# A decoder layer on one core: routing, expert weights and the first chunk's expert products moved into the last turns of the context attention

## The chip, the core and the metric

One core of one Trainium2 chip runs the whole kernel. The metric is the device time of one launch in microseconds (us). The kernel before took 2490.17 us, the median of 3 runs (2486.51 to 2495.47). About 0.3% of it, some 7 us, is what a measurement of this kernel can tell from no change. The engines are called PE (TensorE, with its weight loads PEld), DVE (VectorE), ACT (ScalarE), POOL (GpSimd) and SP (SyncE, which issues all transfers here). Each runs its own list of instructions in order. They wait for each other with semaphores.

## What is computed

For each of 2 batches of 2048 tokens of width 512, three steps follow one another, each added to its input:

```
x = x + attention(layernorm(layernorm(x)))                  # 8 heads of 64, normalised q and k
x = x + context_attention(layernorm(x), ctx, ctx)           # 16 heads of 32, 128 context tokens
h = layernorm(x)
idx = top_2(h[:, 0, :] @ Wr + br)                           # two of 8 experts, chosen by token 0 of the batch
x = x + mean over k of (gelu(h @ W1[idx_k] + b1[idx_k]) @ W2[idx_k] + b2[idx_k])
```

All is float32. The kernel splits each operand of a large product into a high and a low float16 part and adds three products, high x high, high x low and low x high. The two experts are the same for all tokens of a batch, and they depend on token 0 of its first chunk alone.

## The kernel before, in words

`decoder_layer` loops over the batches (`nc.Fori(0, B)`). A batch has five stages, each an `nc.Block` in which every engine has its list: projections of the self attention, its scores and values, a short stage that prepares the context's keys and values, the context attention, and the experts. The change touches the last two.

**The context attention** (from L1067) works on 4 chunks of 512 tokens (`CH`), each 4 tiles of 128 (`TPC`). It is a software pipeline of bodies `body(c)`, c = 0 to 4, written out without a loop, and with a list of its own for each engine. Body c holds the attention of chunk c, the output projection of the self attention and the queries of chunk c+1, and the output projection of chunk c-1. The order in which PE calls the pieces is the order in the list. `transposes(kind, c, j)` (L1257, or L888 for "t5") turns one tile of 128 x 512 into a bank of PSUM with 4 matrix instructions. Kind "t5" is the self attention's output, "t0" the normalised input of the queries, "t2" the context attention's output, "t3" the normalised input of the experts. ACT copies the high half out (`high`, L1503), DVE subtracts for the low half (`low`, L1628). `attn_project`, `query` and `cross_project` are products of 12 matmuls of 128 x 128 by 512 each (`mm3`, L159 to L161), as a rule four of them to a chunk. `maxima` (L1300, L1652) and `max_rows` (L1308) find and place the row maxima of the scores. For each of 4 groups of heads g, `scores(c, g)` (L1324) fills four banks, ACT takes the exponential of each pair twice (`exponentials`, L1541 and L1542), POOL subtracts (`probs_low`, L1153), PE multiplies with the values (`values`, L1340 to L1344) and DVE divides by the sums (`output`, L1665 and L1669). `scores` of the next group waits for that division (`d_o`), as it writes the same four banks. `residual2` (L1635, with statistics L922 and L925) adds a projected tile to x, `norm_scale` (POOL, L910 to L917) and `layer_norm` (ACT, L1510) normalise it for "t3". Two banks (TB) serve the transposes and maxima in turn, two (PB) the projections; the order of turns is written in `T_TURNS` and `P_TURNS`, and each turn waits for the reader of the turn two before.

**The experts** (L1790 to L1943) begin when that block has ended. DVE adds the two halves of token 0's column (L1906), PE multiplies with the router's weights (L1841), DVE adds the bias and finds the two largest (L1908 to L1914), SP reads the two indices into registers (L1801) and only then issues the weights: four matrices of 512 x 512, two for `w1` and two for `w2`, in 8 pieces of 128 x 1024 (`load_pieces`, L132), through four slots of `stage_f`. For each piece ACT writes the high half (`split_high`, L140), DVE the low half (`split_low`, L148). Pieces 0 to 3 are the `w1` matrices. The second biases are added to x on POOL (L1835). Then, for each chunk, PE makes 8 products of 12 matmuls from the chunk's "t3" tiles (L159 to L161), ACT takes the gelu (L1894), DVE splits the result into `gh` (L1930) and `gl` (L1932), and PE makes 4 tiles of 24 matmuls each (L1871 to L1875), which DVE adds to x (L1943) and SP writes out. In chunk 0 the splitting of pieces 2 to 7 stands between the gelus; `pe.Fori(0, CH)` runs over the chunks.

## Time and profile before

| | us |
|---|---|
| median of 3 runs (lowest, highest) | 2490.17 (2486.51, 2495.47) |
| the profiled execution, its own time | 2491.35 |
| its span, first to last instruction | 2489.7 |
| PE busy | 2236.2 (90%) |
| DVE, ACT, POOL busy | 1553.7, 1614.5, 1486.8 |
| batch 2: last bodies 2 to 4 of the context attention | 2176.6 to 2294.8 |
| batch 2: routing and first weights | 2294.8 to 2307.3 |
| batch 2: experts of chunk 0, of chunks 1 to 3 | 2307.3 to 2361.8, to 2486.2 |

A row of the profile names the line of the kernel, the engine, the operation, and output <- input. In a line of the timeline the first number is the start in us from the span's start, the second the duration, and the brackets behind it the idle time of the engine before it and who ended that. Matmuls overlap: one of 512 columns is shown with 0.38 us, while the next starts 0.22 us after it. PEclk (and "clock") is the granted clock of TensorE as a share of 2.4 GHz; its two levels are 1.2 GHz (0.50) and 2.4 GHz (1.00), and a stretch shows their mean.

### The profile page before, as it was taken

Reading aid. Unit: us, or ns where it says so; the run is one execution under the profiler, and the core shown is the slowest. Engines: PE = TensorE matmul, PEld = TensorE weight load, DVE = VectorE, ACT = ScalarE, POOL = GpSimd, SP = SyncE. Lnnn points to the kernel's source line nnn. Section 1 sums busy time; section 2 is a strip of 40 time slices with the busy share of each in tenths; the row PEclk is TensorE's granted clock in tenths of the full one; section 3 lists DMA queues with packets and bytes.
Section 4 is the critical chain, followed back from the end, with each engine's and each line's share of the span. In section 5 each row is a group of like instructions: output and inputs, shape, how many; then the busy total and the mean of one; then the engine's idle time right before and its main releaser. Section 6 shows DMA issues by size and latency. Waiting matters only on the chain. (4 is left out here: it accounts for less than half of the span.)

```text
span 2489.7 us, 65787 instructions
## 1 busy us (share of the span) xinstructions
PE 2236.2 (90%) x22384; PEld 1272.3 (51%) x22384; DVE 1553.7 (62%) x2583; ACT 1614.5 (65%) x1828; POOL 1486.8 (60%) x978
## 2 busy tenths in 40 slices
PE   6988999999996899589969889999999968995899
PEld 3544666666663455334435446666666634553344
DVE  6986777777755566353269867777777555663532
ACT  4555999999995556421045469999999945564210
POOL 3325898988985676340033258988989956763400
PEclk9998999999998999789979889999999979997899
DMA  4220000000003000020042200000000030000300
GB/s 102 56 38 1 10 2 6 9 9 8 9 9 106 10 2 2 18 77 17 34 107 56 34 2 10 9 0 9 9 8 9 9 115 1 2 1 15 80 17 34
DMA packets 103502, 65.14 MB, mean 26 GB/s; under 512 B 76498, under 2 KB 76498, under 8 KB 103378
## 3 DMA queue, kind: packets, MB, share of 16 engines
q1 hardware_dynamic: 103378, 63.57, 12.1%
q8 instruction: 68, 1.11, 0.2%
q14 instruction: 56, 0.46, 0.1%
HBM read 46.69 MB, written 8.39 MB: 22 GB/s over the span
## 5 line engine op out<-in xcount | busy, mean ns | idle before, releaser
L668 POOL TENSOR_TENSOR probs_l<-probs,probs_h 128x1024 f16<-128x1024 f32 x448 | 980.4, 2215 | 166.1 <-PE bank L720 127.6
L789 DVE TENSOR_REDUCE pm<-bank 128x1 f32<-128x512 f32 x1024 | 680.5, 688 | 276.8 <-PE bank L676 272.4
L772 ACT ACTIVATE probs_h<-bank,shift 128x1024 f16<-128x1024 f32 x512 | 569.4, 1112 | 51.9 <-PE bank L692 51.9
L780 ACT ACTIVATE probs<-bank,shift 128x1024 f32<-128x1024 f32 x512 | 572.6, 1118 | 34.6 <-DVE probs_l L803 30.3
L691 PE MATMUL bank<-q_hh,ko 128*128 (+1 forms) x1024 | 392.0, 383 | 29.5 <-DMA q_lm<-nm 17.1
L676 PE MATMUL bank<-ko,q_hh 128*128 (+1 forms) x1024 | 397.0, 391 | 21.0 <-PEq L313 12.4
L692 PE MATMUL bank<-q_lm,k_h 65*128 (+1 forms) x1024 | 392.0, 383 | 0.0
L705 PEld LDWEIGHTS bank<-v_hl,probs_h 128*128 128x128 f16 x4096 | 288.1, 98 | 66.3 <-issue 8.3
L705 PE MATMUL bank<-v_hl,probs_h 128*128 (+1 forms) x4096 | 320.8, 192 | 0.8 <-ACT probs_h L772 0.8
L707 PE MATMUL bank<-v_hl,probs_h 128*128 (+1 forms) x4096 | 318.8, 193 | 0.0
L707 PEld LDWEIGHTS bank<-v_hl,probs_h 128*128 128x128 f16 x4096 | 268.1, 96 | 59.1 <-issue 0.5
L720 PEld LDWEIGHTS bank<-v_hl,probs_l 128*128 128x128 f16 x4096 | 187.2, 97 | 57.3 <-POOL probs_l L668 5.1
L1894 ACT ACTIVATE g<-bank,b1c 128x512 f32<-128x512 f32 x64 | 44.1, 689 | 260.5 <-PE bank L161 244.9
L720 PE MATMUL bank<-v_hl,probs_l 128*128 (+1 forms) x4096 | 207.6, 193 | 4.6 <-POOL probs_l L668 4.6
L390 POOL TENSOR_SCALAR rs_a<-mv_a 128x1 f32<-128x1 f32 x32 | 6.2, 192 | 318.4 <-DMA lnb<-in_L_attn_ln_beta 181.7
L1153 POOL TENSOR_TENSOR pxl<-px,pxh 128x1024 f16<-128x1024 f32 x64 | 135.2, 2132 | 58.8 <-ACT px L1542 58.6
L676 PEld LDWEIGHTS bank<-ko,q_hh 128*128 (+1 forms) x1024 | 100.3, 98 | 126.2 <-DVE pm L789 33.4
L691 PEld LDWEIGHTS bank<-q_hh,ko 128*128 (+1 forms) x1024 | 99.7, 97 | 94.6 <-DMA q_lm<-nm 18.1
L692 PEld LDWEIGHTS bank<-q_lm,k_h 65*128 (+1 forms) x1024 | 99.9, 98 | 65.0 <-issue 3.0
L159 PE MATMUL bank<-x2th,fwh_w 128*128 x256 | 100.9, 394 | 29.3 <-DVE fwl_w L148 29.3
L475 ACT ACTIVATE sq<-bank 128x512 f32<-128x512 f32 x64 | 38.3, 599 | 120.8 <-PE bank L161 120.8
L1652 DVE TENSOR_REDUCE nmt<-bank 128x4 f16<-128x512 f32 x128 | 81.7, 692 | 55.5 <-PE bank L1300 54.6
(204 smaller groups left out, 4157.8 us busy)
## 6 DMA issues: line engine op xcount, KB each, us to landing
xt_a<-in_x SPq DMA_DIRECT2D x32, 256.0 KB, 2.7
q_lm<-in_x SPq DMA_DIRECT2D x32, 256.0 KB, 4.6
stage_f<-in_L_ffn_W SPq DMA_DIRECT2D x32, 256.0 KB, 4.8
out<-yt_f SPq DMA_DIRECT2D x32, 256.0 KB, 2.0
q_hh<-q_hh SPq DMA_DIRECT2D x32, 128.0 KB, 2.5
ko<-k_h SPq DMA_DIRECT2D x32, 128.0 KB, 2.7
q_lm<-nm SPq DMA_DIRECT2D x256, 0.2 KB, 4.9
v_hl<-in_L_attn_w_q SPq DMA_DIRECT2D x8, 256.0 KB, 7.0
```

The source lines that it names most:

```text
L159: pe.matmul(bank, xh(c), wh(c), start=(c == 0), stop=False)
L668: pool.tensor_tensor(probs_l[:, p % 2, :], probs[:, p % 2, :], probs_h[:, p % 4, :], ALU.subtract).then_inc(pl_pool, 1)
L676: pe.matmul(MB[k % 2], qf[:, bass.ds(r * CT + k // 4 * P, P)], k1[:, bass.ds(r // CH * N + k % 4 * CT, CT)], start=True, stop=True)\
L691: pe.matmul(bank, k1[:, kcols], qf[:, qcols], start=True, stop=False)
L692: mm = pe.matmul(bank, k2[0:DH + 1, kcols], lf[0:DH + 1, qcols], start=False, stop=True)
L705: pe.matmul(ob[:, o0:o0 + DH + 1], rows, vf[:, bass.ds(v0, DH + 1)], start=(p == 0 and half == 0 and t == 0), stop=False, skip_group_check ...
L707: pe.matmul(ob[:, o0:o0 + DH], rows, vf[:, bass.ds(v0 + DH + 2, DH)], start=False, stop=False, skip_group_check=True)
L720: mm = pe.matmul(ob[:, o0:o0 + DH + 1], probs_l[:, p % 2, half * CT + t * P:half * CT + t * P + P], vf[:, bass.ds(v0, DH + 1)], start=Fals ...
L772: act.activation(probs_h[:, p % 4, :], SB[p % 2][:, :], ACT.Exp, bias=shift[:, 0:1]).then_inc(ph_ready, 1)
L780: act.activation(probs[:, p % 2, :], SB[p % 2][:, :], ACT.Exp, bias=shift[:, 0:1]).then_inc(p_ready, 1)
L789: dve.tensor_reduce(pm[:, s, k:k + 1], MB[k % 2], AX_X, ALU.max).then_inc(mx_free, 1)
L1153: pool.tensor_tensor(pxl[:, k % 2, :], px[:, k % 2, :], pxh[:, k % 2, :], ALU.subtract)\
```

## The change

The block of the experts is gone. Its work stands in the lists of the context attention. Bodies 0 and 1 stay as they are; bodies 2 to 4 are replaced by one list for each engine, in which are interleaved:

- the column of token 0, the routing product (`route`) and the choice (`column`, `choose`) near the beginning of body 2's work, since chunk 0's "t3" tiles are ready by then;
- the loads of the weights, by SP, once the last "t5" transpose has read the self attention's output: its memory between the outputs of the chunks holds `stage_f`, `b2r` and `b2s` (`o_gap`). The split halves go where dead matrices and tiles lie (`fwh`, `fwl`: the weights "o" and "xq", and `oth`, `otl`, `xth`, `xtl`), and wait therefore for the last attention projection (pieces 0 to 3) or the last query (4 to 7);
- the 8 first products of chunk 0 (`expert_up`) on PE: one behind `values(3, 1)`, two behind `scores(3, 2)`, two behind `scores(3, 3)`, one behind `values(3, 6)`, two behind `values(3, 7)`. They share the banks PB with the projections. DVE copies each from its bank to float32 in memory (`expert_raw`, new work), and ACT takes the gelu from there, after all exponentials, so that its tables are loaded once a batch as before;
- the 4 second products of chunk 0 (`expert_down`) behind the last projection, and the last three "t3" transposes behind these. The loops of all engines then run over chunks 1 to 3. Before its loop PE waits for the low half of the last "t3" tile (`d_tl`).
- On POOL, three of four additions of the second bias for chunk 0 (`add_b2`) stand between `norm_scale(1, 2, 1)` and `probs_low(3, 2)`; `query_low(3, 3)` stands behind `probs_low(3, 3)`, `add_xbo(3, 2)` and `add_xbo(3, 3)` behind `probs_low(3, 7)`. The additions for chunks 1 to 3 wait for `gl` of the chunk before.

The diff, cut to its core (indented less than in the file):

```diff
+b2r = [o_gap(i, 2 * D, D) for i in range(2)]
+b2s = [o_gap(2 + i, 2 * D, D) for i in range(2)]
+fwh = {"w10": wh["o"], "w11": oth, "w20": wh["xq"], "w21": xth}
+fwl = {"w10": wl["o"], "w11": otl, "w20": wl["xq"], "w21": xtl}
+g32 = q32
+raw = [tok0, tokx[0]]
+yt = [bo_b, xbo_b]
+def gh(k, ec):
+    return raw[k][:, ec, :].bitcast(F16)[:, 0:CT]
+def gl(k, ec):
+    return raw[k][:, ec, :].bitcast(F16)[:, CT:2 * CT]
 SB = banks[0:4]
 TB = banks[4:6]
...
+    sp.wait_ge(d_t_done, T_BASE + t_of("t5", CH - 1, TPC - 1) + 1)
+    sp.nop(nofuse=True)
+    load_pieces(sp, b, PIECES_P4[:4], stage_f, src)
+    for k in range(2):
+        sp.dma_start(b1c[:, k, :], b1[bass.ds(expert[k], 1), :, :].rearrange("a p c -> p (a c)"))\
+            .then_inc(f_b, 16)
+        sp.dma_start(b2r[k], b2[bass.ds(expert[k], 1), :].broadcast_to([P, D])).then_inc(f_b, 16)
+    load_pieces(sp, b, PIECES_P4[4:], stage_f, src)
+    with sp.Fori(0, CH) as c:
...
+    def add_b2(c, j):
+        n = b * CH + c
+        pool.wait_ge(f_b2, 2 * b + 2)
+        pool.wait_ge(d_n1, n * TPC + j + 1)
+        pool.tensor_tensor(x2_tile(c, j), x2_tile(c, j), b2s[1], ALU.add).then_inc(f_xb, 1)
...
+    add_b2(0, 3)
+    norm_scale(pool, 1, 3, 3)
+    pool.wait_ge(d_n1, (b * CH + CH) * TPC)
+    pool.nop(nofuse=True)
+    with pool.Fori(1, CH) as c:
+        n = b * CH + c
+        pool.wait_ge(f_gl, n * 8)
...
+    def route():
+        pe.wait_ge(r_col, b + 1)
+        bank = bank_free("rt", 0, 0)
+        for d in range(DC):
+            mm = pe.matmul(bank[0:1, 0:E], col[:, d:d + 1], wr_sb[:, d, :], start=(d == 0),
+                           stop=(d == DC - 1))
+        mm.then_inc(r_mm, 1)
+    def expert_up(w):
+        k, ec = w // DC, w % DC
+        if w == 0:
+            pe.wait_ge(d_tl, T_BASE + t_of("t3", 0, TPC - 1) + 1)
+        if ec == 0:
+            pe.wait_ge(w_split, pieces_split(b, PIECES_P4[:2 * k + 2]))
+        ecols = slice(ec * P, ec * P + P)
+        mm3(pe, bank_free("f1", 0, w), lambda d: fwh[f"w1{k}"][:, d, ecols],
+            lambda d: fwl[f"w1{k}"][:, d, ecols], lambda d: x2th[:, d, 0:CT],
+            lambda d: x2tl[:, d, 0:CT]).then_inc(f1_done, 1)
+    def expert_down(n, j):
+        if j == 0:
+            pe.wait_ge(d_o, (b * CH + CH) * 8)
+            pe.wait_ge(w_split, pieces_split(b, PIECES_P4))
+        pe.wait_ge(f_y, n * TPC + j + 1)
+        cols = slice(j * P, j * P + P)
+        bank = SB[j % 2][:, :]
+        for w in range(8):
+            k, ec = w // DC, w % DC
+            if j == 0:
+                pe.wait_ge(f_gl, n * 8 + w + 1)
+            pe.matmul(bank, gh(k, ec)[:, cols], fwh[f"w2{k}"][:, ec, :], start=(w == 0),
+                      stop=False)
+            pe.matmul(bank, gh(k, ec)[:, cols], fwl[f"w2{k}"][:, ec, :], start=False, stop=False)
+            mm = pe.matmul(bank, gl(k, ec)[:, cols], fwh[f"w2{k}"][:, ec, :], start=False,
+                           stop=(w == 7))
+        mm.then_inc(f2_done, 1)
...
+    max_rows(3)
+    transposes("t2", 2, 1)
+    scores(3, 0)
+    cross_project(2, 0)
+    cross_project(2, 1)
+    transposes("t2", 2, 2)
+    transposes("t2", 2, 3)
+    values(3, 0)
+    values(3, 1)
+    expert_up(0)
+    scores(3, 1)
+    cross_project(2, 2)
+    transposes("t3", 2, 0)
+    cross_project(2, 3)
+    values(3, 2)
+    values(3, 3)
+    transposes("t3", 2, 1)
+    scores(3, 2)
+    expert_up(1)
+    expert_up(2)
+    values(3, 4)
+    transposes("t3", 2, 2)
+    values(3, 5)
+    transposes("t3", 2, 3)
+    scores(3, 3)
+    expert_up(3)
+    expert_up(4)
+    values(3, 6)
+    expert_up(5)
+    values(3, 7)
+    expert_up(6)
+    transposes("t2", 3, 0)
+    expert_up(7)
+    transposes("t2", 3, 1)
+    cross_project(3, 0)
+    transposes("t2", 3, 2)
+    transposes("t2", 3, 3)
+    cross_project(3, 1)
+    cross_project(3, 2)
+    transposes("t3", 3, 0)
+    cross_project(3, 3)
+    expert_down(b * CH, 0)
+    expert_down(b * CH, 1)
+    expert_down(b * CH, 2)
+    expert_down(b * CH, 3)
+    transposes("t3", 3, 1)
+    transposes("t3", 3, 2)
+    transposes("t3", 3, 3)
+    pe.wait_ge(d_x2, (b * CH + CH) * TPC)
+    pe.wait_ge(f_raw, b * 8 + 8)
+    pe.wait_ge(d_tl, T_BASE + len(TILES))
+    pe.nop(nofuse=True)
...
+    def weights_high(p):
+        if p < 4:
+            act.wait_ge(d_o_done, (b * CH + CH) * TPC)
+        else:
+            act.wait_ge(d_q_done, (b * CH + CH) * DC)
+        split_high(act, b, PIECES_P4[p:p + 1], stage_f, fwh)
+    def gelu(w):
+        k, ec = w // DC, w % DC
+        if w == 0:
+            act.wait_ge(d_ql, (b * CH + CH) * DC)
+            act.wait_ge(f_b, b * 64 + 64)
+        act.wait_ge(f_raw, b * 8 + w + 1)
+        if w >= 2:
+            act.wait_ge(f_gl, b * (CH * 8) + w - 1)
+        act.activation(g32[:, w % 2, :], raw[k][:, ec, :], ACT.Gelu, bias=b1c[:, k, ec:ec + 1],
+                       scale=INV_WS).then_inc(f_g, 1)
...
+    exponentials(3, 0)
+    exponentials(3, 1)
+    high("t2", 2, 2)
+    high("t2", 2, 3)
+    weights_high(7)
+    layer_norm(1, 2, 0)
+    exponentials(3, 2)
...
+    exponentials(3, 6)
+    exponentials(3, 7)
+    high("t3", 2, 3)
+    act.preload_act_table(ACT.Gelu)
+    gelu(0)
+    gelu(1)
+    gelu(2)
+    gelu(3)
+    high("t2", 3, 0)
+    gelu(4)
+    high("t2", 3, 1)
+    gelu(5)
+    high("t2", 3, 2)
+    gelu(6)
+    layer_norm(1, 3, 0)
+    gelu(7)
+    high("t2", 3, 3)
+    layer_norm(1, 3, 1)
+    layer_norm(1, 3, 2)
+    high("t3", 3, 0)
+    high("t3", 3, 1)
+    high("t3", 3, 2)
+    layer_norm(1, 3, 3)
...
+    def column():
+        dve.wait_ge(d_tl, T_BASE + t_of("t3", 0, 0) + 1)
+        dve.tensor_tensor(col[:, :], x2th[:, :, 0], x2tl[:, :, 0], ALU.add).then_inc(r_col, 1)
+    def choose():
+        dve.wait_ge(r_mm, b + 1)
+        dve.tensor_tensor(sc[:, :], proj_bank("rt", 0, 0)[0:1, 0:E], br_sb[:, :], ALU.add)\
+            .then_inc(r_sc, 1)
+        dve.wait_ge(r_sc, b + 1)
+        dve.nop(nofuse=True)
+        dve.max(best[:, :], sc[:, :]).then_inc(r_top, 1)
+        dve.wait_ge(r_top, b + 1)
+        dve.nop(nofuse=True)
+        dve.max_index(idx[:, :], best[:, :], sc[:, :]).then_inc(r_idx, 1)
+    def weights_low(p):
+        if p < 4:
+            dve.wait_ge(d_o_done, (b * CH + CH) * TPC)
+        else:
+            dve.wait_ge(d_q_done, (b * CH + CH) * DC)
+        split_low(dve, b, PIECES_P4[p:p + 1], stage_f, fwh, fwl)
+    def bias2():
+        dve.wait_ge(f_b, b * 64 + 64)
+        dve.tensor_tensor(b2s[0], b2r[0], b2r[1], ALU.add).then_inc(f_b2, 1)
+        dve.wait_ge(f_b2, 2 * b + 1)
+        dve.tensor_scalar(b2s[1], b2s[0], 0.5, None, ALU.mult).then_inc(f_b2, 1)
+    def expert_raw(w):
+        k, ec = w // DC, w % DC
+        if w == 0:
+            dve.wait_ge(d_t_done, T_BASE + t_of("t0", CH - 1, TPC - 1) + 1)
+        elif w == 4:
+            dve.wait_ge(d_t_done, T_BASE + t_of("t3", CH - 2, TPC - 1) + 1)
+        dve.wait_ge(f1_done, b * (CH * 8) + w + 1)
+        dve.tensor_copy(raw[k][:, ec, :], proj_bank("f1", 0, w)).then_inc(f_raw, 1)
+    def expert_split(n, w):
+        k, ec = w // DC, w % DC
+        dve.wait_ge(f_g, n * 8 + w + 3)
+        dve.tensor_copy(gh(k, ec), g32[:, w % 2, :]).then_inc(f_gh, 1)
+        dve.wait_ge(f_gh, n * 8 + w + 1)
+        dve.tensor_tensor(gl(k, ec), g32[:, w % 2, :], gh(k, ec), ALU.subtract).then_inc(f_gl, 1)
+    def result(n, c, j):
+        cols = bass.ds(c * (TPC * D) + j * D, D)
+        dve.wait_ge(f2_done, n * TPC + j + 5)
+        dve.wait_ge(f_xb, n * TPC + j + 1)
+        dve.wait_ge(y_out[j % 2], n * 32 + 16 * (j // 2) + 16)
+        dve.wait_ge(d_xb, (b * CH + CH) * TPC)
+        dve.wait_ge(d_xb2, (b * CH + CH) * TPC)
+        dve.scalar_tensor_tensor(out=yt[j % 2][:, :], in0=SB[j % 2][:, :], scalar=0.5 * INV_WS,
+                                 in1=x2[:, cols], op0=ALU.mult, op1=ALU.add).then_inc(f_y, 1)
...
+    maxima(3, 15)
+    low("t2", 2, 0)
+    low("t2", 2, 1)
+    bias2()
+    weights_low(3)
+    residual2(2, 0)
+    residual2(2, 1)
+    low("t2", 2, 2)
+    output(3, 0)
+    output(3, 1)
+    weights_low(4)
+    low("t2", 2, 3)
+    expert_raw(0)
+    weights_low(5)
+    residual2(2, 2)
+    output(3, 2)
+    output(3, 3)
+    residual2(2, 3)
+    expert_raw(1)
+    low("t3", 2, 0)
+    weights_low(6)
+    low("t3", 2, 1)
+    output(3, 4)
+    output(3, 5)
+    expert_raw(2)
+    low("t3", 2, 2)
+    weights_low(7)
+    expert_raw(3)
+    low("t3", 2, 3)
+    expert_raw(4)
+    output(3, 6)
+    expert_split(b * CH, 0)
+    expert_raw(5)
+    output(3, 7)
+    expert_split(b * CH, 1)
+    expert_split(b * CH, 2)
+    expert_raw(6)
+    low("t2", 3, 0)
+    expert_split(b * CH, 3)
+    expert_raw(7)
+    low("t2", 3, 1)
+    expert_split(b * CH, 4)
+    residual2(3, 0)
+    low("t2", 3, 2)
+    expert_split(b * CH, 5)
+    residual2(3, 1)
+    low("t2", 3, 3)
+    expert_split(b * CH, 6)
+    expert_split(b * CH, 7)
+    residual2(3, 2)
+    residual2(3, 3)
+    result(b * CH, 0, 0)
+    result(b * CH, 0, 1)
+    low("t3", 3, 0)
+    low("t3", 3, 1)
+    low("t3", 3, 2)
+    result(b * CH, 0, 2)
+    result(b * CH, 0, 3)
+    low("t3", 3, 3)
```

## Rows read from the trace of the kernel before

**Rows 1.** The page: busy time of PE, and its granted clock in 40 slices.

```profile
PE 2236.2 (90%) x22384; PEld 1272.3 (51%) x22384; DVE 1553.7 (62%) x2583; ACT 1614.5 (65%) x1828; POOL 1486.8 (60%) x978
...
PEclk9998999999998999789979889999999979997899
```

**Rows 2.** Windows: length, busy us (and instructions) of each engine, clock.

```profile
core 0: us, PE busy (x) PEld busy (x) DVE busy (x) ACT busy (x) POOL busy (x), PEclk, DMA share, GB/s
2176.60:2229.80 53.20, 50.02 (x469) 27.43 (x466) 35.34 (x70) 33.42 (x47) 34.98 (x41) 1.00 0.01 2
2229.80:2267.50 37.70, 25.46 (x292) 14.44 (x292) 15.61 (x35) 22.86 (x29) 18.74 (x19) 0.82 0.00 1
2267.50:2294.80 27.30, 19.64 (x128) 11.22 (x128) 12.77 (x24) 7.58 (x12) 6.66 (x14) 0.75 0.00 1
2294.80:2307.30 12.50, 0.37 (x9) 0.26 (x9) 3.31 (x8) 2.43 (x3) 0.00 (x0) 0.50 0.65 161
2307.30:2339.20 31.90, 24.91 (x96) 10.22 (x97) 26.62 (x21) 12.15 (x15) 26.09 (x16) 0.87 0.36 86
2339.20:2361.80 22.60, 22.60 (x97) 9.93 (x98) 3.89 (x7) 0.00 (x0) 0.00 (x0) 0.92 0.10 36
2361.80:2486.20 124.40, 124.29 (x576) 56.13 (x574) 35.17 (x60) 16.52 (x24) 0.00 (x0) 1.00 0.07 25
930.70:1116.30 185.60, 144.33 (x1096) 73.91 (x1095) 99.09 (x164) 78.59 (x106) 87.94 (x90) 0.86 0.12 31
```

**Rows 3.** Waits of PE from 2229.8 to 2312: total us, times, longest.

```profile
PE bank L159 <- DVE fwl_w L148: 11.6, 1, 11.6
PE bank L1340 <- POOL pxl L1153: 10.2, 4, 4.4
PE bank L1324 <- DVE ko L1669: 3.3, 3, 2.0
```

**Rows 4.** Timeline, all engines: one group's turn from scores to the next scores.

```profile
2241.96 0.40 PE L1324 MATMUL bank<-qh,kth 32*128 32x512 f16 x4 [0.45 <-DVE ko L1669]
...
2243.20 1.02 ACT L1541 ACTIVATE pxh<-bank 128x1024 f16<-128x1024 f32 x1 [0.36 <-PE bank L1324]
...
2245.23 4.24 POOL L1153 TENSOR_TENSOR pxl<-px,pxh 128x1024 f16<-128x1024 f32 x2 [0.18 <-ACT px L1542]
...
2251.96 0.42 DVE L1669 TENSOR_TENSOR ko<-bank,rd 128x256 f32<-128x256 f32 x1
...
2252.44 0.40 PE L1324 MATMUL bank<-qh,kth 32*128 32x512 f16 x4 [2.05 <-DVE ko L1669]
```

**Rows 5.** Timeline: last t3 tile, column, first weight piece, table load, first product.

```profile
2292.29 1.11 PE L1257 MATMUL bank<-ident,ko 128*128 128x128 f32 x4 [2.37 <-ACT ko L1510]
...
2294.07 0.69 DVE L1628 TENSOR_TENSOR x2tl<-bank,x2th 128x512 f16<-128x512 f32 x1 [0.70 <-ACT x2th L1503]
2295.07 0.17 DVE L1906 TENSOR_TENSOR col<-x2th,x2tl 128x4 f32<-128x4 f16 x1 [0.31 <-PEq L1076]
...
2302.50 1.06 ACT L140 ACTIVATE fwh_w<-stage_f 128x1024 f16<-128x1024 f32 x1 [8.47 <-DMA stage_f<-in_L_ffn_W]
2306.98 1.28 ACT L1884 ACT_TABLE_LOAD   x1 [1.10 <-DMA b2r<-in_L_ffn_b]
...
2307.28 0.61 PE L159 MATMUL bank<-x2th,fwh_w 128*128 x1 [11.64 <-DVE fwl_w L148]
```

**Rows 6.** Timeline of DVE: the same steps beside POOL's additions, and without them.

```profile
2319.06 1.64 DVE L1932 TENSOR_TENSOR gl<-g,gh 128x512 f16<-128x512 f32 x1
2320.63 2.28 DVE L148 SCALAR_TENSOR_TENSOR fwl_w<-stage_f,fwh_w 128x1024 f16<-128x1024 f32 x1
...
2336.67 0.42 DVE L1930 CAST gh<-g 128x512 f16<-128x512 f32 x1
2337.13 0.69 DVE L1932 TENSOR_TENSOR gl<-g,gh 128x512 f16<-128x512 f32 x1
2337.74 1.22 DVE L148 SCALAR_TENSOR_TENSOR fwl_w<-stage_f,fwh_w 128x1024 f16<-128x1024 f32 x1
```

## Prediction: routing, weights and chunk 0's expert products inside the context attention

> **What bounds the kernel now.** I read the page first: PE is busy 90% of the span, and its clock dips in the same places of both batches [rows 1]. So the question is not which engine is busiest but where PE has no work. The windows answer it [rows 2]. Body 2 is dense: 50.0 of 53.2 us busy at clock 1.00. From `max_rows(3)` to the last exponential (37.7 us) PE is busy 25.5 us at clock 0.82; from there to the last "t3" tile (27.3 us) 19.6 us at 0.75; in routing and loading (12.5 us) hardly at all; the first products of chunk 0 take 31.9 us, its second ones 22.6. Chunks 1 to 3 run at 124.4 us for 576 matmuls, 0.216 us each, with nothing left to gain. From body 2 to the end of chunk 0 batch 2 needs 185.2 us (the first six windows), batch 1 185.6 us (the last window); batch 1 repeats the pattern, so I cost one batch and double.
>
> Why does PE idle there? The waits [rows 3] name three causes. One wait of 11.6 us for the split weights: "t3" must be done, then come column, choice, loads, splits, from 2294.07 to 2307.28 [rows 5]. Four waits, 10.2 us, for POOL's low parts of the exponentials, and three, 3.3 us, for the division. These last two are one chain [rows 4]: scores at 2241.96, exponentials from 2243.20, POOL's two subtractions from 2245.23 for 4.24 us, values, division from 2251.96, next scores at 2252.44: 10.5 us a group, while PE has half of that in work. In chunk 3 no queries follow that could fill it. The third loss is in chunk 0: DVE is busy 26.6 of 31.9 us, since beside POOL's 26.1 us of additions its steps are stretched, a weight split 2.28 us against 1.22, a `gl` 1.64 against 0.69 [rows 6].
>
> **The change, part by part**, with A = body 2's work, B = `max_rows(3)` to the last exponential, C = from there to the first second product (`expert_down`), D = the four second products, E = from their end to the first matmul of chunk 1. Before: A 53.2; B 37.7; the rest 94.3 [rows 2].
>
> *Removed*: 12.5 us of routing and loading, and the 31.9 us of first products as a stage of their own. Their 96 matmuls are 20.7 us of PE work at 0.216.
>
> *A.* PE gains only the routing product, 0.37 us [rows 2]. SP's loads have 16 issues and wait for nothing else in SP's list; before, the first piece was ready for ACT 7.4 us after the column [rows 5], and now 20 us or so of other work covers that. DVE gains the column, 0.17 [rows 5], and a choice of four instructions as small, 0.7, and three splits: 35.3 + 0.9 + 3 x (1.22 to 2.28) = 39.9 to 43.0 us. ACT gains seven high halves at 1.06: 33.4 + 7.4 = 40.8. POOL loses three steps. All stay under 53, but the lists are in order and DVE is what paces the 16 maxima at the end, where two of the splits stand: PE waits behind them. Bounds: nothing, or all three splits at 2.28 less the cover, 6. I take 2.8, so A = 56.0.
>
> *B.* The chain of rows 4 stays. Gain: six products (15.5 us) fill PE, 25.5 us at 0.82 being 20.9 at full clock, so 36.4 of work: the clock should stay at 1.00, worth a us or two in the scores. Cost: `expert_up(0)` lies between `values(3, 1)` and `scores(3, 1)`, 2.6 us where PE waits 2.05 us for the division in any case [rows 4], so 1 us; the other five stand under exponentials and POOL's work, cover of 5 us and more a group. POOL gains three additions (26.1 for 16, 1.6 each) and a `query_low` ahead of chain steps: 18.7 + 4.9 + 1.2 = 24.8 us, but 4.9 in one gap of about 5.5 together with two `norm_scale`: 1 us late, perhaps 3. The additions wait for `bias2` on DVE; behind them in POOL's list waits `probs_low(3, 2)`, behind that `values(3, 2)`. DVE gains five splits, the biases (about 1.1), and copies out of PSUM. The copy is not in the trace; the nearest are DVE's steps out of PSUM of this size at 0.69, and a cast at 0.42 from memory; I take 0.69, five of them 3.5: 15.6 + 1.1 + 3.5 + 5 x (1.22 to 2.28) = 26.3 to 31.6 us, under 40. `weights_high(7)` makes ACT wait for a load that begins after `weights_low(3)`, with `exponentials(3, 2)` behind it: asked for about 5 us into B (my estimate from DVE's list), and ready at most 7.4 us later, as the first piece was behind its column [rows 5]: 12.4 us, against 13.4 us when those exponentials began before (2243.20), so no stall, or up to 2 us. B = 40.0 (38 to 45).
>
> *C.* PE: two products 5.2 us, `cross_project(3, *)` 10.4, five transposes at about 0.6, half of the 1.11 seen at the low clock [rows 5], 2.8: 18.4. DVE: 12.8 us of before, less three low halves (2.1, now in E), and eight splits of gelu at 1.07 from start to start [rows 6], 8.6, and three copies, 2.1: 21.4. ACT loads its table first, 1.28 us [rows 5], which was behind the loads before and is now ahead of `gelu(0)`, with `expert_split(0)` behind it on DVE, and the second products behind that. So DVE sets C, not PE: 21.4 plus the first gelu's latency, 23.0 (21 to 25.5).
>
> *D.* 96 matmuls, 20.7; with a clock step 21.0 (20.8 to 22; before 22.6).
>
> *E.* New, with no cover. PE's loop waits for the last "t3" low half. From that tile's transposes to the end of its low half is 2.5 us (2292.29 to 2294.76) [rows 5]; the third tile's bank waits for the first one's low half, and two results of 0.69 us stand between on DVE. One latency, 2.5, is the lower bound, two with the results 6.4, plus a clock dip the upper. E = 6.0 (4 to 7.5).
>
> *Chunks 1 to 3*: same instructions, 124.4. POOL's additions for them fall under the second products, when DVE splits nothing.
>
> Sum: 56.0 + 40.0 + 23.0 + 21.0 + 6.0 = **146.0** a batch against 185.2 and 185.6: 39.2 and 39.6 less, together 78.8. The profiled execution took 2491.35 us, so 2412.5; the median of the runs lies 1.2 below it: **2411**.
>
> **The Trainium skill.** Beside POOL's additions a split takes 2.28 us, 1.06 more than without [rows 6]. "SBUF — State Buffer", section "Who interferes with whom", says of a DVE instruction with two SBUF inputs beside a GpSimd one that the second to issue "fully blocks until the first finishes". Against this change that rule is the first rival below: the new neighbours are POOL's subtractions, which are longer than its additions. "ScalarE: Activation LUTs", section "What ACT_TABLE_LOAD costs", adds some 1.4 us of drain to the load; the trace shows the load's 1.28 alone, and by the page the estimate of the sum would be 2.8 us more over both batches, 2414.
>
> **Rivals.**
> 1. *POOL and DVE lock each other out.* Each of eight splits waits for a whole subtraction (2.12, half of 4.24 [rows 4]), 17.0 us, and each delays one by 1.22, 9.8 us; 26.8 less the 5.1 in A and B is 21.7 more: 167.7 a batch, 35.4 saved, **2456**. For it: each step beside POOL is about 1 us longer [rows 6]. Against: POOL is idle a third of A and half of B, and the stretch shown there is half of this.
> 2. *The products don't fit among the scores.* All six delay the chain instead of lying beside it: B = 37.7 + 15.5 = 53.2, 159.2 a batch, **2438**. For: each is 2.6 us in an ordered list. Against: waits of 4.4 us stand there [rows 3].
> 3. *PE alone decides.* A 50.4; B and C 20.9 + 14.7 + 20.7 = 56.3; D 20.7; E 2.5: 129.9 a batch, 2379; with a little idle time up to 2394. Against: A left 3 us idle even before, and the sum of DVE in C.
> 4. *Slower than before.* The wait in E lets the clock fall, and it stays at 1.2 GHz over the loop's beginning, where every matmul takes twice 0.216. Such time costs itself again; from 39.4 us of full-speed work on (182 matmuls) the gain is gone. Over the whole of chunk 1 (41.5 us) it is 2.1 a batch too much, **2495**. Before, routing and loading ran at 0.50 for 12.5 us, and yet the next stage had 0.87 [rows 2], so the clock comes back in a few us.
>
> **How the numbers follow.** Forecast 0.73 for 2394 to 2438 without rival 2; rival 2 0.08, near the upper end; rival 1 0.10, above; rival 3 0.07, below; rival 4 0.02. The low ends 53.5 + 38 + 21 + 20.8 + 4 = 137.3 give 96 us less, 2394; the high ends 59 + 45 + 25.5 + 22 + 7.5 = 159.0 give 53 less, 2438. The range leaves out 0.19. Faster by over 0.3% (7 us, what a measurement of this kernel can tell from no change): 0.97; within it 0.01, a part of rival 4's case; slower 0.02.
>
> **What would show it.** In the trace after: no window near clock 0.50 ahead of the experts; the first weight load issued inside body 2's work; group turns of chunk 3 at 10 to 11 us (rival 2: 13); splits at 1.2 to 2.3 us (rival 1: over 3, with POOL's subtractions over 2.13); DVE busy over 85% of C; a gap of about 6 us on PE ahead of chunk 1 (rival 4: matmuls 0.43 us apart long behind it). If A grows by more than 6 us, or C passes 27, my reading of DVE's ordered list was too kind.

## Result: 2413 us, against 2411 forecast

On one chip the changed kernel took 2412.97 us, the median of four runs (2405.34 to 2413.87), and the kernel before 2489.82 (four runs, 2486.51 to 2495.47): a ratio of 0.9682, 95% interval 0.9656 to 0.9709. On another chip the same pair gave 2412.30 and 2495.26, ratio 0.9672 (0.9656 to 0.9688). The time lies inside the forecast range, 2394 to 2438, and 2 us from the forecast value. The profiled execution took 2413.03 us, with a span of 2411.4 against 2489.7.

The page of the changed kernel, first lines and the clock, to be held against [rows 1]:

```profile
PE 2222.3 (92%) x22384; PEld 1264.9 (52%) x22384; DVE 1542.9 (64%) x2599; ACT 1611.7 (67%) x1828; POOL 1481.4 (61%) x978
...
PEclk9997999999999899999979979999999998999999
```

PE's instructions are the same number, and its busy time is 14 us less, the time that matmuls were stretched at the low clock. The rest of the 78 us is, for the most part, waiting that is gone. From [rows 2] and the windows below, batch 2 had 39 us of PE idle between the start of B and the start of chunk 1 (12.2, 7.7, 12.1 and 7.0 in the four windows before the second products), and has 7 now (3.9 in B, 3.3 in E); PE's busy time there fell from 93.0 to 81.0 us.

The windows of batch 2 after, in the order A, B, C, D, E, chunks 1 to 3 (columns as in [rows 2]: us, busy us and instructions of PE, PEld, DVE, ACT, POOL, clock, DMA):

```profile
2138.80:2193.70 54.90, 51.63 (x481) 27.70 (x478) 40.60 (x79) 39.89 (x54) 33.32 (x38) 1.00 0.32 78
2193.70:2233.40 39.70, 35.77 (x345) 18.51 (x344) 25.46 (x43) 23.35 (x30) 25.43 (x23) 0.96 0.05 15
2233.40:2256.20 22.80, 22.80 (x160) 12.19 (x158) 19.98 (x36) 10.91 (x17) 7.38 (x10) 1.00 0.00 1
2256.20:2276.90 20.70, 20.70 (x97) 9.44 (x96) 4.39 (x9) 1.29 (x2) 3.33 (x7) 1.00 0.07 27
2276.90:2281.90 5.00, 1.70 (x13) 1.21 (x11) 3.18 (x5) 2.38 (x4) 2.13 (x2) 0.94 0.16 62
2281.90:2407.60 125.70, 125.68 (x576) 56.69 (x576) 34.48 (x59) 16.49 (x24) 12.66 (x11) 0.99 0.06 25
```

The window with clock 0.50 and the products' window with DVE at 26.6 of 31.9 us [rows 2] have no counterpart. PE is busy in all of C and D. The windows' edges are set by hand; the table has the stages from one event to the next (us), taken from the same start and end instructions in every trace. In the runs it repeats within 0.1 us where neither order nor work was changed, except B, where the clock's dips fall differently (38.4 to 39.75), and chunks 1 to 3 behind an E of 5 us (124.3 to 126.0, last section).

| Stage | before, batch 1 / 2 | forecast | after, both |
|---|---|---|---|
| A | 53.4 / 53.4 | 56.0 | 55.1 |
| B | 36.3 / 37.7 | 40.0 | 39.75 |
| C | 72.1 / 71.7 with routing and first products | 23.0 | 22.55 |
| D | 22.4 / 22.4 | 21.0 | 20.9 |
| E | 0 | 6.0 | 5.0 |
| sum | 184.2 / 185.2 | 146.0 | 143.3 |
| chunks 1 to 3 | 124.3 | 124.4 | 125.7 |

### The profile page after: what moved, and what is told of

It reads as the page before. It is cut to its first block and busy times, and to the rows that moved or that the text cites. A ratio compares the mean times of both kernels' runs of the same rounds, so it can differ in the third digit from the quotient of the medians.

```text
span 2411.4 us, 65807 instructions
## 1 busy us (share of the span) xinstructions
PE 2222.3 (92%) x22384; PEld 1264.9 (52%) x22384; DVE 1542.9 (64%) x2599; ACT 1611.7 (67%) x1828; POOL 1481.4 (61%) x978
## 3 DMA queue, kind: packets, MB, share of 16 engines
q1 hardware_dynamic: 103378, 63.57, 12.3%
## 5 line engine op out<-in xcount | busy, mean ns | idle before, releaser
L677 PE MATMUL bank<-ko,q_hh 128*128 (+1 forms) x1024 | 397.1, 391 | 20.8 <-PEq L314 12.3
L677 PEld LDWEIGHTS bank<-ko,q_hh 128*128 (+1 forms) x1024 | 100.3, 98 | 126.0 <-DVE pm L790 33.4
L2032 ACT ACTIVATE q<-bank,b1c 128x512 f32<-128x512 f32 x48 | 33.0, 687 | 181.1 <-PE bank L161 181.1
L1359 POOL TENSOR_TENSOR q_lm<-q_lm,ko 128x512 f32 x24 | 29.6, 1264 | 152.9 <-DVE ko L2130 116.3
L2064 DVE TENSOR_REDUCE nmt<-bank 128x4 f16<-128x512 f32 x128 | 81.9, 690 | 55.1 <-PE bank L1435 54.1
```

The source lines that it names most:

```text
L677: pe.matmul(MB[k % 2], qf[:, bass.ds(r * CT + k // 4 * P, P)], k1[:, bass.ds(r // CH * N + k % 4 * CT, CT)], start=True, stop=True)\
L2064: dve.tensor_reduce(nmt[:, j, d::32], tile_bank("sm", c, i).rearrange("p (a k) -> p a k", k=CTX), AX_X, ALU.max, negate=True).then_inc(d_n ...
```

## What the experiments tell apart

The first theory: what was saved is made of the products laid beside the scores and of the removed stage of routing and loading; A is DVE's, C is DVE's, E has no cover. The rivals: the first products cost as much in the chain as they save, and the locks between POOL and DVE carry what is left. Stage times below are from one profiled execution each; the whole time wanders by some microseconds between runs of one kernel, for a reason told further down, so the stages carry the verdicts.

**The products put behind the scores.**

The edit, cut to PE's list, several calls to a line:

```
-  values(3, 1); expert_up(0); scores(3, 1)
-  scores(3, 2); expert_up(1); expert_up(2); values(3, 4)
-  scores(3, 3); expert_up(3); expert_up(4); values(3, 6); expert_up(5); values(3, 7)
+  scores(3, 3); values(3, 6); values(3, 7); expert_up(0) ... expert_up(5)
```

DVE's copies and splits of the products go behind `output(3, 7)`, and the last two `cross_project` pieces of chunk 2 go ahead of the first product in the order in which the banks PB are taken (`TAIL_P`, the list of turns).

> The changed kernel with one part undone: routing and weights stay early, but the six first products that stood among the scores of chunk 3 (expert_up 0 to 5) come behind values(3, 7), and their copies on DVE with them. Theory (the products fill idle time of PE): stage B stays near 38 to 39.5 us, and C grows from 22.8 by the five products that were in B, 13 us, to about 36; D and E stay. Some 12 us a batch, so 2413 + 24 = 2437, up to 2443 if the clock dips in B again. Rival (DVE's list paces C, and PE waits in B were not worth much): C grows only by the five copies, 3.5 us, to 26.5, 2420. Second rival (the products already lengthened the chain of groups as they stood): B falls by 5 us or more when they leave.

It took 2441.03 us, inside the 2437 to 2443 expected, against 2493.84 for the kernel before on that chip. Its windows B and C of batch 2:

```profile
2208.40:2246.30 37.90, 25.30 (x290) 14.13 (x288) 21.78 (x39) 23.47 (x30) 25.84 (x23) 0.84 0.06 15
2246.30:2283.70 37.40, 35.78 (x212) 17.99 (x213) 21.89 (x40) 10.97 (x16) 7.31 (x10) 0.93 0.01 1
```

B is again what it was before, 25.3 us busy at clock 0.84 [rows 2]. C grows from 22.55 to 37.4 and 37.8. The sum is 158.1 and 156.3 a batch, 14.7 and 13.0 more than after. So of the 15.5 us of PE work in six products, 13 to 15 are saved by their place beside the scores, and the other two thirds of what a batch gains (26 to 29 of 41 to 42 us) are what is left for the routing and loading moved away, and the additions with them. That share is found by subtraction; no run undoes it alone. Rival 2 has no room here: B is 37.9 and 39.3 us without the products and 39.75 with them, 0.5 to 1.9 us more for 15.5 us of work.

**Every low split done twice.** (The code is shortened.) Each of the eight splits gets a second instruction of the same kind and size ahead of it, into memory that nothing reads; beyond this only that memory and a semaphore are added.

```
+  dve.wait_ge(jk, b * 8 + p + 1)
+  dve.scalar_tensor_tensor(out=junk[:, :, :], in0=stage_f[...], scalar=WS, in1=fwh[name][:, part, :],
+                           op0=ALU.mult, op1=ALU.subtract).then_inc(jk, 1)
   split_low(dve, b, PIECES_P4[p:p + 1], stage_f, fwh, fwl)
```

> The changed kernel with the low half of each weight piece computed twice on DVE, the first time into memory that nobody reads: eight more splits of 1.22 us a batch, 9.8 us of DVE, each with two inputs from memory. Theory (DVE has slack in B; in A two of the three splits stand among the maxima, where DVE paces PE): A grows by 2 to 3 us, B by 0 to 2, 2413 + 7 = 2420. Rival 1 of the prediction (POOL and DVE lock each other out): each added split also waits for a subtraction or delays one, A and B grow by 10 us or more a batch, 2433 or above, and many splits take over 2 us. Rival of no effect: all of it is hidden, 2413 to 2415.

It took 2435.75 us, 23 more than after. The stages: A 62.2 and 59.3, B 43.6 and 43.3, C 24.0 and 24.2, D and E as they were: 12.5 and 9.3 a batch, for eight instructions of 1.22 us (9.8). A with three extra splits (3.7 us) grew by 4.2 and 7.1. PE's waits in A and B of batch 2 (total us, times, longest):

```profile
PE bank L1477 <- POOL pxl L1226: 4.3, 4, 2.0
PE bank L1437 <- DVE x2tl L2042: 3.1, 1, 3.1
PE bank L1437 <- DVE nmt L2066: 1.9, 5, 1.1
```

and POOL's subtractions that ran beside them:

```profile
2190.33 3.11 POOL L1226 TENSOR_TENSOR pxl<-px,pxh 128x1024 f16<-128x1024 f32 x1
2202.39 4.67 POOL L1226 TENSOR_TENSOR pxl<-px,pxh 128x1024 f16<-128x1024 f32 x2 [1.62 <-ACT px L1841]
2214.85 5.14 POOL L1226 TENSOR_TENSOR pxl<-px,pxh 128x1024 f16<-128x1024 f32 x2 [7.78 <-ACT px L1841]
```

The first of these three rows is not the doubling's: the kernel after has the same single subtraction of 3.11 us, at 2177.29. The pairs of 4.67 and 5.14 us are; the same pairs take 4.21 and 4.23 after. DVE ahead of the 3.1 us wait:

```profile
2189.48 1.97 DVE L2112 SCALAR_TENSOR_TENSOR junk<-ko,dwh_o 128x1024 f16<-128x1024 f32 x1
2191.38 3.14 DVE L148 SCALAR_TENSOR_TENSOR dwl_o<-ko,dwh_o 128x1024 f16<-128x1024 f32 x1
2194.45 0.68 DVE L2042 TENSOR_TENSOR x2tl<-bank,x2th 128x512 f16<-128x512 f32 x1
```

The low half that PE waits for stands behind two splits of one piece, which took 5.1 us beside POOL's subtraction from 2190.33, where two undisturbed ones take 2.4. So the longest wait is a locked split in DVE's list, and rival 1's mechanism is at work here. The 16 instructions took 27.0 and 25.2 us a batch, against 12.3 for the eight after: 14.7 and 12.9 more, and not 9.8. A third part is the clock, 0.92 and 0.97 in A against 1.00, with PE busy 54.9 and 53.0 us against 51.7. The time is above the 2433 that the expectation set for rival 1, and A and B together grew by 11.0 and 7.7 us where it asked for 10; but only four and three of the 16 took over 2 us. The first theory's 2420 was too low, and this run alone would have said that all splits are dear. The next run shows what two of them cost where they stand.

**Splits moved behind the maxima.**

```
-  weights_low(1) behind output(2, 4); weights_low(2) behind maxima(3, 5)
+  weights_low(1), weights_low(2) behind low("t2", 2, 1)
-  weights_high(5), (6) in body 2; weights_high(7) behind high("t2", 2, 3)
+  weights_high(5) there; (6) behind exponentials(3, 3); (7) behind exponentials(3, 5)
```

> The changed kernel with the low halves of weight pieces 1 and 2 moved from among the maxima of chunk 3 to the start of stage B, and the high halves of pieces 5 to 7 moved behind, since they wait for the slots. Theory (A is longer than before because DVE's ordered list paces the maxima; doubling the splits made A 4 to 7 us longer): A falls from 55.1 to the 53.4 of before or a little under, B grows by 0 to 1.5 as three splits now stand ahead of residual2(2, 0): between 0 and 2 us a batch, 2409 to 2413. Rival (A is set by PE, 51.6 of 54.9 us busy): A stays at 55.1 and B grows, 2413 to 2418.

It took 2415.20 us. Its windows A and B, and PE's waits in B:

```profile
2137.00:2191.50 54.50, 51.79 (x481) 27.87 (x479) 37.93 (x77) 38.02 (x52) 32.59 (x38) 1.00 0.25 59
2191.50:2234.90 43.40, 36.20 (x345) 18.69 (x344) 32.77 (x45) 25.15 (x32) 26.00 (x23) 0.96 0.16 38
```

```profile
PE bank L1459 <- DVE ko L2081: 2.9, 3, 1.9
PE bank L1475 <- POOL pxl L1224: 2.3, 3, 1.3
PE bank L159 <- DVE q_lm L2047: 1.0, 1, 1.0
```

A is 54.52, 0.6 less. B is 43.43, 3.7 more: DVE's work there goes from 25.5 to 32.8 us, and the division (`ko`) comes late. The two splits among the maxima cost 0.6 us, and nearly the whole of that place was free. The 2.8 us of my forecast were not there, though A came out within 1 us of it. The time is in the rival's range (2413 to 2418), A between the marks of the two.

Why B pays 3.7 us for two splits of 1.22 is in DVE's rows. The three splits behind the moved ones, pieces 3 to 5, took 7.4 us here and 3.8 after:

```profile
2199.06 3.15 DVE L148 SCALAR_TENSOR_TENSOR otl<-ko,oth 128x1024 f16<-128x1024 f32 x1
...
2207.46 1.90 DVE L148 SCALAR_TENSOR_TENSOR dwl_xq<-ko,dwh_xq 128x1024 f16<-128x1024 f32 x1
...
2210.48 2.32 DVE L148 SCALAR_TENSOR_TENSOR dwl_xq<-ko,dwh_xq 128x1024 f16<-128x1024 f32 x1
```

The first ran beside a pair of POOL's subtractions (from 2196.27, 4.86 us in place of 4.22), the other two beside its additions of the second bias (`add_b2`, from 2207.02, 4.71 us for three). All eight splits took 15.2 us, against 12.3 after. In this order the lock of rival 1 costs 5.4 us of DVE's time a batch, twice what it costs in the change's order, and the division waits behind it. How the 3.7 us divide between that and the moved splits' own 2.4 no run tells.

**Which engine sets C.** Three runs: less work on PE, less on DVE, and both. The first leaves out the correction terms of products 6 and 7 of chunk 0 (8 of 12 matmuls each); the second takes the statistics of chunk 3's last norm from 64 of 512 columns.

The two edits, cut to their core, the first run's ahead of the dots and the second's behind them:

```
+  if w >= 6:
+      for d in range(DC): mm = pe.matmul(bank, fwh[...][:, d, ecols], x2th[:, d, 0:CT], ...)
...
+  cut = 64 if s == 1 and c == CH - 1 else D
+  dve.bn_stats(st[:, k, :], x2_tile(c, j)[:, 0:cut])
```

> The changed kernel with 8 of 24 matmuls less in each... that is, expert_up 6 and 7 of chunk 0 make only their high x high products, 16 matmuls less a batch, 3.45 us of PE work in stage C. Part of the computation is left out. The prediction said that DVE sets C: then C stays at 22.8 us, within 0.5. Rival (PE sets C, since a fifth product and two values fell into it that the sum had left out): C falls by 3 us or more, to below 20, and the time by 6 us or more, 2406.

> The changed kernel, where the statistics of chunk 3's last layer norm are taken from 64 of 512 columns: four instructions of DVE in stage C of about 0.2 us in place of 0.69, 2 us less a batch. That part of the result is only approximate. With 16 matmuls less (3.45 us) C fell from 22.55 to 21.13, and then PE waited 1.5 us for DVE. Theory now: PE sets C as it stands, and DVE is 1.4 us behind it as the next bound; so less DVE work alone changes nothing: C 22.5 (within 0.2). Rival (the forecast's: DVE sets C): C falls by 1.5 to 2 us.

> Both cuts at once: 16 matmuls less in stage C, and 2 us less of DVE's statistics. Part of the computation is left out, as in the two kernels that it joins. If PE is the first bound of C and DVE the second, C falls below the 21.13 of the matmul cut alone, to 19.1 to 20.2 (22.55 - 3.45 = 19.1 is PE's own bound). If something else came after PE (the gelus' latency, the table load, the copies in turn with the banks), C stays at 21.1.

They took 2404.28, 2406.47 and 2407.36 us. Window C of the first:

```profile
2225.70:2246.80 21.10, 19.52 (x142) 10.37 (x140) 19.25 (x36) 10.81 (x17) 7.48 (x10) 1.00 0.01 2
```

PE's waits in it (total us, times, longest):

```profile
PE bank L159 <- DVE xol L2047: 1.5, 2, 1.4
```

Window C of the second, less on DVE:

```profile
2226.70:2249.10 22.40, 22.40 (x157) 12.13 (x156) 19.11 (x36) 10.85 (x16) 7.32 (x10) 1.00 0.01 1
```

Window C of the third, less on both:

```profile
2230.90:2251.70 20.80, 19.38 (x142) 10.44 (x141) 18.63 (x36) 10.74 (x16) 7.56 (x10) 1.00 0.01 2
```

With 3.45 us less of matmuls (16 at 0.216) C falls from 22.55 to 21.13, and PE now has a wait for DVE of 1.5 us. With about 0.9 us less DVE work alone it falls by 0.1, to 22.45. So PE sets C; not DVE, as I had it: PE waits for nothing in C of the kernel after, and taking work from it shortens C. Neither mark of the first expectation was met (no change within 0.5, or 3 us and more), since C falls by 1.4 of the 3.45 us. The cut on DVE took 0.9 us out of C and not the 2 us that were expected, so it is a weaker test than planned. Right behind PE, at 21.1, another bound stands, and with less on DVE as well (18.6 us busy in place of 19.3) C is 20.8, short of the 19.1 to 20.2 that DVE as the second bound would give. The wait of 1.4 us for DVE's `xol` stands in both runs. I take the second bound for the order of steps, each waiting for the one before it on another engine, and not for DVE's busy time (18.6 of 20.8 us); no run shows that, and which of the steps is the long one was not settled.

**The last "t3" tiles among the second products.**

```
   expert_down(0); expert_down(1)
-  expert_down(2); expert_down(3); transposes("t3", 3, 1); ("t3", 3, 2); ("t3", 3, 3)
+  transposes("t3", 3, 1); ("t3", 3, 2); expert_down(2); transposes("t3", 3, 3); expert_down(3)
```

ACT's and DVE's lists follow: `layer_norm(1, 3, 3)` two places earlier, `low("t3", 3, 0)` ahead of the first `result`, and `low("t3", 3, 3)` ahead of the last.

> The changed kernel with the last three t3 tiles moved from behind the second products of chunk 0 to among them (two behind the second of them, one behind the third), and their halves on ACT and DVE with them. Theory: the 5.0 us of stage E are latency without cover; of them only the transposes' own 1.3 us remain, and the clock dip at the start of chunk 1 (125.5 us against 124.1 before) goes: 5.1 us a batch, 2413 - 10 = 2403. Rival (the latency turns up as a wait in D or at the loop's start instead): within 2 us of 2413. Second rival (the dip comes from the loop's entry, not from the wait): E falls, chunk 1 to 3 stay at 125.5, 2406.

> The changed kernel with the last t3 tiles among the second products, timed. By stages it is 4.1 to 5.1 us a batch shorter and 1.4 us more at the start of chunk 1: 11 to 13 us less than the changed kernel on this chip, a ratio between the two of 0.995. The single run before showed 17 us, of which some 4 would then be the fall of the clock dips elsewhere.

A single run gave 2395.86 us; on another chip the same kernel took 2402.61 (2399.08 to 2405.58), ratio 0.963 (0.9614 to 0.9646), and the changed kernel beside it 2412.30:

> The changed kernel as it is, timed on the same chip as its two variants, so that their difference is a difference of kernels: 2413, give or take 4 us for where the clock dips fall.

Windows C, D and chunks 1 to 3 of batch 2, on that other chip:

```profile
2228.60:2251.20 22.60, 22.60 (x159) 12.08 (x157) 19.78 (x36) 10.93 (x17) 7.40 (x10) 1.00 0.01 1
2251.20:2273.40 22.20, 22.20 (x110) 10.83 (x109) 7.37 (x13) 3.80 (x6) 8.30 (x11) 1.00 0.10 37
2273.40:2397.70 124.30, 124.30 (x577) 56.27 (x575) 35.17 (x60) 16.52 (x24) 9.88 (x8) 1.00 0.07 25
```

D takes 1.3 us more, the transposes, and E is zero. Chunks 1 to 3 are back at 124.3. A batch gains 5.0 + 1.4 - 1.3 = 5.1 us, two 10.2; measured are 9.7, a little under the 11 to 13 last expected. The wait has two parts, then: 5 us of it, and 1.4 behind it. These rows of the changed kernel show how:

```profile
2276.91 1.04 PE L1388 MATMUL bank<-ident,ko 128*128 128x128 f32 x8
...
2278.17 1.29 DVE L2040 TENSOR_TENSOR x2tl<-bank,x2th 128x512 f16<-128x512 f32 x2 [10.14 <-ACT x2th L1800]
...
2279.45 0.65 PE L1388 MATMUL bank<-ident,ko 128*128 128x128 f32 x4 [1.51 <-DVE x2tl L2040]
...
2280.77 0.69 DVE L2040 TENSOR_TENSOR x2tl<-bank,x2th 128x512 f16<-128x512 f32 x1
...
2281.92 0.60 PE L159 MATMUL bank<-x2th,dwh_o 128*128 x1 [1.81 <-DVE x2tl L2040]
2282.32 0.63 PE L160 MATMUL bank<-x2tl,dwh_o 128*128 x1
...
2285.03 0.38 PE L161 MATMUL bank<-x2th,dwl_o 128*128 x1
```

The chain is the forecast one: two transposes, low halves, the third tile held for the first's bank, its low half, then the loop. And its first matmuls stand 0.4 us apart, the 1.2 GHz level, until 2284.8, where they are 0.216 apart again: seven at twice the time, 1.4 us.

**Both moves together.**

> The two rearrangements together: the last t3 tiles among the second products of chunk 0, and the two splits behind the maxima. If they add: D + E 22.25, A 53.4 to 54, chunks 1 to 3 at 124.3; 2396 less 0 to 4, so 2392 to 2396, a ratio to the kernel before of 0.961 to 0.963. If the moved splits only shift the wait into B: 2396 to 2400.

2405.31 us (2403.86 to 2406.34), ratio 0.9646 (0.962 to 0.9672). The stages add up exactly: A 54.52, B 43.43, C 22.55, D 22.25, E 0, 142.75 a batch. B's 3.7 us are kept; with the "t3" move alone the sum is 138.3 to 139.6. The time is outside both ranges of the expectation (2392 to 2396, or 2396 to 2400): they were counted from the single 2395.86. The stages say that the splits belong where the change has them; the two whole times, 0.9646 and 0.963 of the kernel before, have intervals that overlap.

**Scores ahead of the first product**, with the "t3" move.

```
-  values(3, 1); expert_up(0); scores(3, 1)
+  values(3, 1); scores(3, 1); expert_up(0)
```

> The changed kernel with the last t3 tiles among the second products, and in addition scores(3, 1) ahead of expert_up(0) on PE. The prediction priced expert_up(0) at 1 us in B, since it stands in front of the scores that the chain of groups waits for. Theory: the chain gets that back where the division is ready sooner than the product ends: B 0.8 to 1.0 us shorter a batch, 1 to 2 us in all against the kernel with the t3 tiles alone. Rival (B is set by PE's sum, 35.8 of 39.7 us busy): no change within 0.3 us in B, the product only moves.

2399.13 us (2397.67 to 2401.36), ratio 0.9616 (0.9599 to 0.9632), the fastest median of the study. But its interval overlaps that of the "t3" move alone, and the stages show no gain to explain one: B 39.87 against 39.74 and 39.36, sum 139.75 against 139.64 and 139.25. Start of each group's exponentials, the kernel after and then this one:

```profile
2196.37 1.02 ACT L1838 ACTIVATE pxh<-bank 128x1024 f16<-128x1024 f32 x1 [0.89 <-PE bank L1459]
...
2207.29 1.02 ACT L1838 ACTIVATE pxh<-bank 128x1024 f16<-128x1024 f32 x1 [2.36 <-PE bank L1459]
...
2219.08 1.02 ACT L1838 ACTIVATE pxh<-bank 128x1024 f16<-128x1024 f32 x1 [0.95 <-PE bank L1459]
...
2229.65 1.02 ACT L1838 ACTIVATE pxh<-bank 128x1024 f16<-128x1024 f32 x1 [3.27 <-PE bank L1459]
```

```profile
2189.67 1.02 ACT L1838 ACTIVATE pxh<-bank 128x1024 f16<-128x1024 f32 x1 [0.90 <-PE bank L1459]
...
2200.32 1.02 ACT L1838 ACTIVATE pxh<-bank 128x1024 f16<-128x1024 f32 x1 [2.05 <-PE bank L1459]
...
2213.02 1.02 ACT L1838 ACTIVATE pxh<-bank 128x1024 f16<-128x1024 f32 x1 [1.06 <-PE bank L1459]
...
2223.07 1.02 ACT L1838 ACTIVATE pxh<-bank 128x1024 f16<-128x1024 f32 x1 [3.27 <-PE bank L1459]
```

The turns are 10.9, 11.8 and 10.6 us after, and 10.65, 12.7 and 10.05 here. The first is 0.3 us shorter, not 1, and the three together are as long as before (33.3 and 33.4 us). So the theory's 0.8 to 1.0 us are not there, as the rival had it. Whether the 3.5 us between the two medians are more than scatter stays open.

## Why the prediction was right, and where it was only lucky

- **The removed stages**: right. PE's 11.6 us wait for the split weights [rows 3] is gone; the first weight load is issued at 2153.95, 15 us into A, and ACT's first high half at 2163.56 waited for PE, not for the load. The cover held with room.
- **A, 56.0 against 55.1**: the size held, the reason did not. I put 2.8 us on splits among the maxima and the moving of those splits showed 0.6. The rest of the 1.7 us by which A grew I account for, without a run, by the routing product (0.36) and a "t2" transpose that now falls ahead of A's end, with its wait (0.8 of `DVE nmt` for L1388 that A did not have before). PE is busy 51.6 of 54.9 us; it is what mostly sets A.
- **B, 40.0 against 39.75**: right in size, and partly by luck. The recorded terms are not added up to 40.0, and the clock was to stay at 1.00; the 39.75 hold 1.4 us that the low clock cost. In the same kernel on the other chip batch 2 had no dip there:

```profile
2191.30:2229.70 38.40, 34.37 (x345) 18.13 (x344) 23.95 (x43) 23.26 (x30) 26.43 (x23) 1.00 0.06 15
```

  Rows say the chain stayed and the products lie beside it: 35.8 us busy, where I had 36.4. Inside it two terms were wrong and small: `expert_up(0)` ahead of the scores costs its turn 0.3 us and not 1, and the three turns together nothing, and the clock stood at 0.96, not 1.00. DVE was busy 25.5 us, under even my low bound of 26.3.
- **C, 23.0 against 22.55**: the number right, the step wrong. "DVE sets C, not PE" fell: DVE is busy 20.0 us, and PE 22.8 of 22.8 at full clock. My 18.4 us for PE was mis-sized. I counted two products behind the last exponential; the trace has 43 matmuls of products there (3.6 products, 9.3 us against my 5.2), since `expert_up(5)` and part of `expert_up(4)` stand there too, and 48 small matmuls of `values` besides. With them my sum would have been 22.5 us and more. Two errors, one on each engine, met at nearly the same time. The sure sign of which it was is that C has no wait on PE at all.
- **D, 21.0 against 20.9**: right.
- **E, 6.0 against 5.0**: right in mechanism, link by link. What the sum left at nothing, with chunks 1 to 3 at 124.4, is the price behind it: 1.4 us of doubled matmuls in chunk 1, 125.7 against 124.3. It is rival 4's mechanism at a thirtieth of its size.
- **The sum** was 2.7 us too high a batch, 5.4 in all. Three things gave that back: 2.8 for chunk 1; 1.4 because my window of batch 1 before began 1.4 us early (184.2 from the same events, where I read 185.6); and batch 1's body 2 began at 933.7 against 931.9. In all 40.9 + 41.9 saved, less 2.8 and 1.8, is 78.2, and the spans differ by 78.3. The last term is not the change's: body 2 of batch 1 begins anywhere from 928.7 to 935.7 us in the 12 traces of the kernel after and its variants, though nothing ahead of it differs in order or work. To meet the time within 2 us, where one kernel's own times differ by 8, was luck. D and E came out for the reasons given; A, B and C in part by luck.
- **Rival 1, the lock**, exists, at a seventh of its price. DVE's splits in A and B took 1.22, 1.43, 1.57, 1.22, 1.22, 1.32, 3.08 and 1.22 us. Here are an ordinary one and the blocked one, and the subtraction beside it:

```profile
2197.17 1.22 DVE L148 SCALAR_TENSOR_TENSOR otl<-ko,oth 128x1024 f16<-128x1024 f32 x1
...
2223.33 3.08 DVE L148 SCALAR_TENSOR_TENSOR xtl<-ko,xth 128x1024 f16<-128x1024 f32 x1
```

```profile
2221.10 4.22 POOL L1224 TENSOR_TENSOR pxl<-px,pxh 128x1024 f16<-128x1024 f32 x2 [1.02 <-ACT px L1839]
```

  The second of the two subtractions runs from about 2223.2 to 2225.3, and the split that was issued at 2223.33 ends at 2226.4, 1.1 us later, nearly the length of an undisturbed split. All eight together are 2.5 us longer than eight of 1.22, not 17. The reverse is seen once: a single subtraction of 3.11 us against 2.13, at 2177.29, behind a split issued 0.3 us ahead of it. By the Trainium skill, "SBUF — State Buffer", section "Summary: rules for kernel authors", the second to issue "fully blocks until the first finishes"; the trace agrees for the 3.08. (The words stand in that section; "Who interferes with whom", which the prediction names, has the lock and that the order of issue decides.) The same kernel on the other chip has the pair the other way round in batch 2:

```profile
2219.61 1.50 DVE L148 SCALAR_TENSOR_TENSOR xtl<-ko,xth 128x1024 f16<-128x1024 f32 x1
...
2217.90 5.20 POOL L1224 TENSOR_TENSOR pxl<-px,pxh 128x1024 f16<-128x1024 f32 x2 [0.17 <-ACT px L1839]
```

  Here the split was issued first, about 0.4 us ahead of the second subtraction; the split is short, and the pair takes 5.20 in place of 4.22. Who pays, and how much, hangs on tenths of a microsecond and on the order of DVE's list: DVE loses 2.5 us over the eight splits in the first of these traces, 0.9 in the second, 5.4 with two splits moved, and more with all splits doubled.
- **The table load.** "ScalarE: Activation LUTs", section "What ACT_TABLE_LOAD costs", of the Trainium skill adds about 1.4 us of drain. In C the trace does not show it:

```profile
2233.28 0.63 ACT L1800 ACTIVATE x2th<-bank 128x512 f16<-128x512 f32 x1
2233.93 1.28 ACT L2003 ACT_TABLE_LOAD   x1
2235.22 1.33 ACT L1858 ACTIVATE q<-tok,b1c 128x512 f32<-128x512 f32 x2
```

  The load begins 0.02 us behind the instruction before it, and the gelu 0.01 us behind the load. 1.28 us is the whole price.

## What to carry to other kernels

Where a chain of short dependent steps leaves an engine half idle, independent work of the size of its gaps cost almost nothing here: six products of 15.5 us lengthened it by 0.5 to 1.9. Doubling a cost tells what more of it would do, not what it costs now: eight more splits took 9 to 12 us a batch, and moving two away gave 0.6 and took 3.7 elsewhere, as other splits then met POOL's work. Before an instruction with two inputs in memory is moved on DVE, look at what POOL does at its new place. To name the engine that sets a stage, look for its waits before adding up busy times: PE at 22.8 of 22.8 us had none, and the forecast that summed DVE's list named the wrong one.

## What the runs showed that I had not expected

- A wait in a dense stretch is mostly paid again behind it, but not always. The same E of 5.0 us was followed by matmuls at the 1.2 GHz level in seven of the eight traces that have it, at 1.4 to 1.7 us (chunks 1 to 3: 125.7 to 126.0 us); in the one with less work on both engines in C there was none, in either batch (124.3, its matmuls 0.216 us apart from the second on). What that run had otherwise that matters I can't say.
- The whole time of one kernel wanders by up to 8 us (2405.34 to 2413.87), while the stages other than B repeat within 0.1. In the traces the difference lies in where the clock's dips fall: B is 38.4, 39.4 or 39.75 us with the same instructions, and the stretch from the end of batch 1's stages to body 2 of batch 2 took from 932.1 us (the "t3" move, its single run) to 936.7 (the products behind the scores), 936.0 in the kernel before. A single time is therefore a poor witness for a change of 3 us; the table of stages is a good one.
